# A decoder layer on one core: its recurrence scanned in pairs of column blocks

## The reference, cut to what matters

```python
dA = exp(dt[t, d] * A[d, n])                     # A = -exp(A_log)
h[d, n] = h[d, n] * dA + dt[t, d] * B[t, n] * x_conv[t, d]
y[t, d] = h[d, :].sum()                          # then + x_conv * D, * silu(z), @ W_out
```

## Time and profile before

| what | us |
|---|---|
| median of 3 runs | 778.88 (778.17 to 784.62) |
| the profiled execution, its own time | 778.58 |
| its span, first to last instruction | 776.9 |
| busy in the span: PE, DVE, POOL, ACT | 635.3, 582.2, 474.2, 445.6 |
| recurrence, first scan to last gate | 49 to 411 |

### The profile page before, as it was taken

One profiled execution on the slowest core, in us unless ns is written; L12 is line 12 of the kernel. 1 busy time (PEld: TensorE's weight loads), 2 busy tenths in 40 slices (PEclk: granted clock), 3 DMA queues, 4 the chain that ended last, 5 costly groups with the idle time before them and its releaser, 6 DMA issues. The chain is left out here.

```text
span 776.9 us, 10733 instructions
## 1 busy us (share of the span) xinstructions
PE 635.3 (82%) x3130; PEld 397.8 (51%) x3130; DVE 582.2 (75%) x984; ACT 445.6 (57%) x795; POOL 474.2 (61%) x387
## 2 busy tenths in 40 slices
PE   4689875997599975477986999999999898799940
PEld 2233212352133410044545999998989764588830
DVE  5787798799998999999986767587787635444316
ACT  2667798686987888757864354444444310344420
POOL 4169589888998999999844232323354165056550
PEclk9799986999879995599999999999999999999985
DMA  7093144415144444943301132342222179455418
GB/s 204 5 215 70 40 109 108 108 45 132 42 108 109 109 109 108 242 106 81 109 7 49 46 137 78 106 138 100 99 70 70 48 215 293 108 167 147 125 29 310
DMA packets 58294, 87.39 MB, mean 112 GB/s; under 512 B 14101, under 2 KB 43224, under 8 KB 58238
## 3 DMA queue, kind: packets, MB, share of 16 engines
q1 hardware_dynamic: 42686, 67.24, 33.8%
q10 hardware_dynamic: 11616, 10.76, 4.4%
q0 software_dynamic: 3936, 8.72, 3.4%
HBM read 36.54 MB, written 18.66 MB: 71 GB/s over the span
## 5 line engine op out<-in xcount | busy, mean ns | idle before, releaser
L294 POOL TENSOR_TENSOR b_in<-rep,b_rep 128x1024 f32<-128x1024 f32 x128 | 299.0, 2357 | 39.5 <-DVE h L565 32.6
L565 DVE TENSOR_TENSOR_SCAN h<-ps,hlast,b_in 128x512 f32<-128x512 f32 x256 | 306.1, 1262 | 14.8 <-ACT ps L462 8.0
L462 ACT ACTIVATE ps<-rep,neg_a 128x512 f32<-128x512 f32 x256 | 170.9, 684 | 41.9 <-DVE h L565 38.2
L770 PE MATMUL ps<-h,pick 128*32 128x512 f32 x512 | 80.5, 706 | 41.3 <-DVE h L565 41.0
L606 PE MATMUL ps<-xnT,w_in 128*128 128x512 f32 x128 | 68.4, 681 | 10.0 <-ACT xnT L348 4.1
L1064 POOL DMA_INDIRECT rows_by_token<-yt,yrow x46 | 44.8, 975 | 51.5 <-DVE yrow L1410 24.4
L1210 DVE TENSOR_TENSOR p_lo<-ps,p_hi 128x512 fp32r<-128x512 f32 x64 | 35.2, 601 | 35.7 <-ACT p_hi L1075 35.6
L1448 PE MATMUL ps<-v_hi,p_hi 128*128 128x256 f32 x208 | 59.5, 286 | 1.2 <-DVE x_res L1322 1.2
L1448 PE MATMUL ps<-v_lo,p_hi 128*128 128x256 f32 x208 | 58.6, 282 | 0.0
L1448 PE MATMUL ps<-v_hi,p_lo 128*128 128x256 f32 x208 | 58.6, 282 | 0.0
L770 PEld LDWEIGHTS ps<-h,pick 128*32 128x32 f32 x512 | 10.7, 115 | 92.0 <-DVE h L565 81.8
(11 more groups left out here) (254 smaller groups left out, 1306.3 us busy)
## 6 DMA issues: line engine op xcount, KB each, us to landing
rep<-dt_u SPq DMA_DIRECT2D x252, 128.0 KB, 2.4
mask_sb<-in_mask_BxSxS_ik_dram SPq DMA_DIRECT2D x16, 800.5 KB, 4.4
xt<-rows_by_expert SPq DMA_DIRECT2D x46, 129.0 KB
rows_by_token<-pad ACTq DMA_DIRECT2D x4, 1024.0 KB, 4.7
yb<-rows_by_token SPq DMA_DIRECT2D x4, 512.0 KB, 4.7
yb<-rows_by_token ACTq DMA_DIRECT2D x4, 512.0 KB, 5.5
x_res<-in_x_dram SPq DMA_DIRECT2D x1, 1536.0 KB, 8.4
c_raw<-in_ctx_dram SPq DMA_DIRECT2D x1, 1536.0 KB
```

The costliest lines, as they stand in the source:

```text
L294: pool.tensor_tensor(b_in[:, (t - 1) % NB:(t - 1) % NB + 2, :], u_rep[:, n % 2, j - 1:j + 1, :], b_rep[q % 2][:, g, :].unsqueeze(1).to_bro ...
L462: act.activation(psA[:, t % NDA, :], dt_rep[:, n % 2, j, :], ACT.Exp, scale=neg_a[:, k:k + 1]).then_inc(exp_ready, 1)
L565: dve.tensor_tensor_scan(h[:, QC * (s % NH) + j, :], psA[:, t % NDA, :], b_in[:, t % NB, :], hlast[:, k:k + 1], ALU.mult, ALU.add).then_in ...
L770: last = pe.matmul(psY[32 * j:32 * j + 32, :], pick[:, :], h[:, QC * (s % NH) + j, :], start=False, stop=(g == NG - 1))
```

## The change

Two neighbouring tiles (t even and t + 1) are scanned by one instruction of 1024 columns. So that the second tile does not go on from the first one's last state, its factor in column 0 is 0, and its own starting state is put into its input: b_in[0] += factor[0] * hlast. In the first quarter that state is zero. In quarters 1 to 3 ACT does it, with one ACTIVATE of one column per pair (Identity, with hlast as scale and b_in's own column as bias), after waiting for POOL's product of that pair. factor[0] of the second tiles is made apart: POOL computes dt * A for column 0, 4 values per partition, at g = 0 and odd j (24 in all), ACT takes their exponential (24, each followed by a wait for its own end). The exponential of an odd tile leaves out column 0, which DVE has set to zero once. psA becomes a ring of 4 banks, two pairs; the exponential of an even t waits for t - 2 scans, that of an odd one for nothing further. The scan waits for b_ready and exp_ready of both tiles and for the carried state. In the attention part some semaphores are merged, without a change to the order.

```diff
-NB, NDA, NDT, NH = 8, 5, 5, 3
+NB, NDA, NDT, NH = 8, 4, 5, 3
...
+        first_a = sb("first_a", [P, 2, QC // 2, NG])
...
-        psA = ps[:, 3 * BANK:8 * BANK].rearrange("p (s n) -> p s n", s=NDA)
-
-        psL = [psF[:, 0, 0:DM], psF[:, 1, 0:DM]] + [psA[:, t % NDA, 0:DM] for t in (TILES * NQ - 5, TILES * NQ - 4)]
+        psA = ps[:, 3 * BANK:7 * BANK].rearrange("p (s n) -> p s n", s=NDA)
+
+        psL = [psF[:, 0, 0:DM], psF[:, 1, 0:DM], ps[:, 7 * BANK:7 * BANK + DM], psA[:, (TILES * NQ - 4) % NDA, 0:DM]]
... POOL, per tile
+                if g == 0 and j % 2 and q:
+                    if n >= KM + 2:
+                        pool.wait_ge(carried, 8 * (n - KM - 1))
+                    k = t % TILES
+                    pool.tensor_tensor(first_a[:, n % 2, j // 2, :], neg_a[:, k:k + QC * (NG - 1) + 1:QC],
+                                       dt_rep[:, n % 2, j, 0:1].to_broadcast([P, NG]), ALU.mult).then_inc(first_in, 1)
... ACT, per tile
-                if t >= NDA:
-                    act.wait_ge(scanned, t - NDA + 1)
-                act.activation(psA[:, t % NDA, :], dt_rep[:, n % 2, j, :], ACT.Exp,
+                if t >= NDA and t % 2 == 0:
+                    act.wait_ge(scanned, t - NDA + 2)
+                a = t % 2
+                act.activation(psA[:, t % NDA, a:], dt_rep[:, n % 2, j, a:], ACT.Exp,
                                scale=neg_a[:, k:k + 1]).then_inc(exp_ready, 1)
+                if q and t % 2:
+                    pair, g = t // 2 - TILES // 2, k // QC % NG
+                    if g == 0:
+                        e0 = first_a[:, n % 2, j // 2, :]
+                        act.wait_ge(first_in, 2 * (n - KM) + j // 2 + 1)
+                        act.activation(e0, e0, ACT.Exp).then_inc(first_exp, 1)
+                        act.wait_ge(first_exp, 2 * (n - KM) + j // 2 + 1)
+                    act.wait_ge(b_ready, t + 1)
+                    b0 = b_in[:, t % NB, 0:1]
+                    act.activation(b0, first_a[:, n % 2, j // 2, g:g + 1], ACT.Identity, scale=hlast[:, k:k + 1],
+                                   bias=b0).then_inc(carried, 1)
... DVE
+            dve.memset(psA[:, 1:NDA:2, 0:1], 0.0)
...
-                dve.wait_ge(b_ready, t + 1)
-                dve.wait_ge(exp_ready, t + 1)
-                dve.tensor_tensor_scan(h[:, QC * (s % NH) + j, :], psA[:, t % NDA, :], b_in[:, t % NB, :],
-                                       hlast[:, k:k + 1], ALU.mult, ALU.add).then_inc(scanned, 1)
+                if t % 2 == 0:
+                    dve.wait_ge(b_ready, t + 2)
+                    dve.wait_ge(exp_ready, t + 2)
+                    if q:
+                        dve.wait_ge(carried, t // 2 - TILES // 2 + 1)
+                    dve.tensor_tensor_scan(h[:, QC * (s % NH) + j:QC * (s % NH) + j + 2, :].rearrange("p a n -> p (a n)"),
+                                           psA[:, t % NDA:t % NDA + 2, :].rearrange("p a n -> p (a n)"),
+                                           b_in[:, t % NB:t % NB + 2, :].rearrange("p a n -> p (a n)"),
+                                           hlast[:, k:k + 1], ALU.mult, ALU.add).then_inc(scanned, 2)
... PE, at the end
-            pe.wait_ge(scanned, TILES * NQ - 3)
+            pe.wait_ge(scanned, TILES * NQ - 2)
```

More of the change, by code:

```diff
@@ L194, in scan_block @@
         rep_pool = sem("rep_pool")
+        first_in, first_exp, carried = sem("first_in"), sem("first_exp"), sem("carried")
         def rep_sem(n, j):
@@ L887, in attend_and_route @@
         vhi_ready, vlo_ready = sem("vhi_ready"), sem("vlo_ready")
[L888 to L891, removed]
+        xq_ps, xq_ready, q_ps, q_ready, qlo_ready = (
+            sem("xq_ps"), sem("xq_ready"), sem("q_ps"), sem("q_ready"), sem("qlo_ready"))
+        qb_ready = sem("qb_ready")
         filled, scores_ps, masked, nb_ready, exp_done = sem("filled"), sem("scores_ps"), sem("masked"), sem("nb_ready"), sem("exp_done")
@@ L1013, in _ @@
             for par in range(2):
-                pool.memset(pr[:, par, SK:], 0.0).then_inc(pad_zero, 1)
+                pool.memset(pr[:, par, SK:], 0.0).then_inc(consts_made, 1)
             def scatter(c, r):
@@ L1102, in step @@
                     last.then_inc(q_ready, 1)
-                    act.wait_ge(q_ready, i + 1)
-                    act.activation(q_hi[:, (i + 1) % 2, :, :], q[:, (i + 1) % 2, :, :], ACT.Copy).then_inc(qhi_ready, 1)
+                    act.wait_ge(q_ready, 2 * i + 1)
+                    act.activation(q_hi[:, (i + 1) % 2, :, :], q[:, (i + 1) % 2, :, :], ACT.Copy).then_inc(q_ready, 1)
                 par = i % 2
@@ L1112, in step @@
                         act.wait_ge(xq_ps, i)
-                    act.wait_ge(qb_ready, i + 1)
+                    act.wait_ge(qb_ready, 2 * i + 1)
                     act.wait_ge(rstd2, 3 * i + 4)
@@ L1119, in step @@
                     if i < 2:
-                        act.wait_ge(pad_zero, 2)
+                        act.wait_ge(consts_made, 4)
                     else:
@@ L1340, in step @@
                     dve.reduce_max(mx[:, par:par + 1], sc[:, par, :], AXX).then_inc(dve_link, 1)
-                    dve.wait_ge(qb_ready, i + 1)
+                    dve.wait_ge(qb_ready, 2 * i + 1)
                     dve.wait_ge(dve_link, i + 1 + min(i + 1, NT - 2))
-                    dve.tensor_tensor(full[:, :], mx[:, par:par + 1], qb[:, :], ALU.add).then_inc(full_ready, 1)
-                    dve.wait_ge(full_ready, i + 1)
+                    dve.tensor_tensor(full[:, :], mx[:, par:par + 1], qb[:, :], ALU.add).then_inc(qb_ready, 1)
+                    dve.wait_ge(qb_ready, 2 * i + 2)
                     dve.tensor_scalar(nb[:, par:par + 1], qb[:, :], full[:, 0:1], SCALE, ALU.subtract, ALU.mult).then_inc(nb_ready, 1)
                 if on(i, 1) and i >= 0:
-                    dve.wait_ge(qhi_ready, i + 1)
+                    dve.wait_ge(q_ready, 2 * i + 2)
                     dve.tensor_tensor(q_lo[:, (i + 1) % 2, :, :], q[:, (i + 1) % 2, :, :],
@@ L1527, in step @@
                     if on(i, 0):
-                        pe.wait_ge(q_ready, i)
+                        pe.wait_ge(q_ready, 2 * i)
                     x3_transposed(i - 3)
```

## The result

The changed kernel takes 797.39 us (median of 4 runs, 796.27 to 798.65) against 779.22 for the kernel before, measured beside it. The ratio is 1.0225, with a 95% interval of 1.0188 to 1.0262: slower by 2.3%. The forecast was 798. Its profiled execution has a span of 795.4 us, 18.5 more than before. The gate after the last scan starts at 429.76 us; before it started at 410.84. The recurrence holds the whole difference; what follows it takes 365.6 us, where it took 366.1.

What follows compares the result with a forecast made beforehand. The prediction took DVE to bound the recurrence, with ACT a follower running ahead. Its terms, -12.8 + 20.3 + 10.2 + 3 - 3 + 2 = +19.7 us on 778.6, gave 798 us, range 774 to 812.

Steps and rivals of the forecast that it cites:

- The gain: DVE's scans in the recurrence: one instruction per pair saves a fixed part of 0.10 us, 12.8 us over 128 pairs.
- The carry: ACT's new one-column ACTIVATE per pair in quarters 1 to 3: 0.40 us, 0.30 from start to start, 96 of them.
- The lead: ACT's lead over DVE's scans: the longest ACT work that costs DVE nothing falls from 4.4 us to 1.1.
- The rule: Allowance for ACT work between exponentials: scan time of the banks ahead less ACT's fills; 4.4 us before, 1.1 after.
- Silus: Seven ACT lumps of 4.52 us in quarters 0 to 2 stop DVE's scans for longer: +20.3 us.
- rival 1: Faster: lead does not matter, lumps fall into DVE's pauses in the recurrence; 765 us, or 771; chance 0.16.
- The step-size stretch: Six pairs from k = 100 in quarters 1 and 2, and quarter 0's stretch, wait for ACT: +10.2 us.
- Smaller terms: In the recurrence: ACT's evacuations and quarter 3's preparations +3 us, gates -3, POOL level with DVE +2.
- The gates: DVE's waits at gates, 16.3 us before, shrink as stalls give PE time: 3 us taken back (0 to 6).
- Rival 2: No difference within 1%: scan saving of 20 us or carry of 0.1 us on ACT; 783 to 786 us; chance 0.19.
- Rival 3: Slow: POOL loses its lead, ACT's carries wait for its products, PE's front work comes late; 819 us; chance 0.07.
- Rival 4: A pair's scan on DVE is not cheaper, 2.36 us or more, so the saving goes; 811 us; chance 0.06.

Runs made afterwards that it cites:

- the four kernels with single scans: The kernel before, and it with four single banks (788.24 us), four given back in pairs (811.15 us), or three single banks (816.61 us), instead of five.

## Why the prediction was right

**The gain.** Taken at 12.8 us. From start to start it is 128 x (2 x 1.175 - 2.244) = 13.6. The prediction's 1.18 is a little long, because it counts the end of the last of the sixteen scans. The Trainium skill, "DVE: opcode table, instruction layouts, handler registers and perf-mode slots", section on the datapath, has the scan at half throughput, and the trace now agrees with that: 512 columns more cost 2.244 - 1.175 = 1.07 us, and two cycles each would be 1.07. But DVE did not get all of the 13.6 back. The scans' busy time fell by 11.8, from 306.1 to 294.3, and that of DVE as a whole by 9.0. An instruction behind a wait shows its whole length and overlaps with nothing, and DVE now waits 58 times where it waited 21 times. So this term of the sum was 3.8 us too favourable.

**The carry.** Taken at 0.40 and 0.30 from start to start; the rows have 0.377, and the next exponential starts 0.28 later (236.31 to 236.59). The small exponentials took 0.19.

**The lead.** The step on which the forecast rested held: a shorter lead alone slows the kernel before, and most of the waits after are where the rule puts them. The rule, bank releases less ACT's own work, ordered the four kernels with single scans rightly (4.4, 3.2, 2.0, 2.0 us of allowance: 778, 788, 811, 817 us). It did not give the size for the last two, and it does not order single scans against pairs: with 1.1 us of allowance the changed kernel takes 797, less than the 811 of single scans with 2.0, because its scans are cheaper and its sums meet a longer scan.

**Silus.** +20.3 forecast. The seven stalls after are 4.72, 3.58, 2.97, 1.28, 4.76, 1.28 and 4.28, together 22.9 against 9.5: **+13.4**. Two terms were mis-sized. The Silus of xc in quarters 1 and 2 cost 1.28 each, not 3.4, because DVE has four residuals among the scans of just that stretch, about 1.3 us of work that the rule left out, and waits 0.4 and 0.7 us at them for PE; rival 1 was right at this place. And in the packed first quarter the first two stalls were 4.7 and 3.6, not 6.2. Before the change a lump of 4.52 already cost 3.6 there, so only about 0.9 us of lead was at hand, and 2.6 could not be lost. Those of zs were 0.4 to 0.9 longer than forecast.

**The step-size stretch.** +10.2 forecast. In quarter 1 the stalls from 201 to 220 us sum to 4.58 against the 4.8 worked out, in quarter 2 to 3.8. In quarter 0 it was 4.6 against 3.7 before, so +0.9 in place of +2.6. Together 13.0 against 5.7: **+7.3**. The six pairs of quarter 1 took 21.3 us, from 201.07 to the start of the next pair, where the prediction had about 21.

**Smaller terms.** Forecast +3 for evacuations and preparations, 0 to 10. Scans waited for ACT 42.0 us in all; less the Silus (22.9) and 6.2 in the step-size stretches that leaves 12.9, where it was 2.1: **+10.8**, just past the upper end. About 5.6 of it stand in quarter 3, at single waits of 0.4 to 1.8 behind the preparations. The gates gave back 16.3 - 11.8 = **4.5** where 3 was taken. POOL made scans wait 0.3 us, not 2. The residuals waited 1.1 us for PE, and the sum had no such term. Within the gates, the last one's wait rose from 2.9 to 5.2. PE waits there for ACT's evacuation of the query's transpose, one of the last preparations, and has the projections behind it. It stood still at this place before, too, and nearly as long:

```profile
L743 PE MATMUL ps<-xqT,wqk 128*128 128x128 f32 x8 | 1.1, 284 | 3.0 <-ACT xqT L416 3.0
```

What changed is when it comes out of the wait. PE goes on with the states 5.2 us before the end of the last scan (419.14 and 424.30), where it was 7.2 us (400.50 and 407.67), and from there it needs 10.6 us to the gate, where it needed 10.3. PE's timeline after (start, us, idle before), with the projections that the last states wait behind:

```profile
417.16 2.04 PE L769 MATMUL ps<-xqT,wqk 128*128 128x128 f32 x8 [3.36 <-ACT xqT L424]
419.14 1.94 PE L796 MATMUL ps<-h,pick 128*32 128x512 f32 x8
421.00 3.91 PE L660 MATMUL ps<-w_out,zs 128*128 128x256 f32 x12
...
425.84 2.86 PE L660 MATMUL ps<-w_out,zs 128*128 128x256 f32 x12
428.63 1.07 PE L796 MATMUL ps<-h,pick 128*32 128x512 f32 x8
```


**Sum.** From 48 us to just before the last gate's end DVE's busy time fell from 328.4 to 319.4 us and its idle time rose from 35.1 to 63.1: -9.0 + 28.0 = 19.0, against 18.9 at the last gate. The forecast's +19.7 came out this close because its errors cancel. It had 7 us too much at the Silus, 3 at the step sizes, 1.5 at the gates and 1.7 at POOL. It had 8 too little at the small evacuations, 4 at DVE's saving, and 1 at the residuals. The runs show that a short lead costs this kernel time and that the carries hold 7.0 us of the distance; that the total came out to 1 us is luck.

**The rivals.** Rival 1 (the lead does not matter) fell, apart from the residuals. Rival 2 needed a saving of 20 us or a carry of 0.10, and the rows have 13.6 and 0.377. Rival 3's wait for POOL behind the carries is 0.8 us in all. Rival 4 fell with the 2.24 us.

## What to carry to other kernels

- When a change makes a producer's buffers fewer or coarser, work out the longest lump of the producer that the consumer does not feel: the releases ahead, times the consumer's step, less the producer's own fill time on both sides of the lump. Do it for every lump in the producer's queue. Here 9 us less work in the bounding engine was paid for with 28 us more of waits.
- Look for places where the two engines meet outside the ring, such as a sum that needs the other's result: they can cost more than the lumps do (23.6 us at twelve sums with three banks). Without the sums and two ACTIVATEs for each, the kernel before was 2% faster.
- When errors of single terms are as large as the answer, add up the terms after the run as well. A total that fits says little on the terms.

## What the runs showed of the hardware

A scan of 1024 columns with both inputs in SBUF took 3.57 us on the mean beside POOL's products (2.32 to 4.57) and 2.33 with one input in PSUM, with POOL's own products going from 2.36 to 2.80 on the mean. Where such a scan took 2.34, POOL's instruction beside it was the longer one (3.24 us instead of 1.27). A scan of 1024 columns whose factors lie in two PSUM banks costs 2.24 us from start to start, 0.11 less than two of 512 (1.175 each).
